# Layer 3's self attention: the weights' sums held in 8 rows a head, inverted in 128 columns and spread by a 0/1 product

## What is computed

```python
g = sigmoid(hidden_states @ Wg + bg)
res = (1.0 - Z_I) * maximum(1.0 - Z_I - Z_J, 0.0) + Z_I * minimum(1.0 - Z_I + Z_J, 1.0)
scope = clip(power(base, 1.0 - g) + 2.0 - abs_ij, 1e-32, 1.0)
log_pen = log(maximum(res * scope, 1e-32))
scores = einsum('bhqd,bhkd->bhqk', q, k) / sqrt(HEAD_DIM) + log_pen[:, None]
probs = softmax(scores, axis=-1)
ctx = einsum('bhqk,bhkd->bhqd', probs, v)
x = layernorm(x + ctx)
```

## Time and profile before

| What | Value |
|---|---|
| median of 3 runs | 2808.49 us (2806.22 to 2809.91) |
| the profiled execution's own time | 2809.17 us |
| its span, first to last instruction | 2807.3 us |
| mean granted TensorE clock | 0.928 |
| PE busy | 2396.4 us (85%) |
| PE weight loads busy | 1887.2 us (67%) |
| DVE busy | 1402.2 us (50%) |
| ACT busy | 871.3 us (31%) |
| POOL busy | 675.7 us (24%) |
| reciprocals of this stage (L2341) | 32, from 2159.3 to 2421.4 us, 55.8 us in all |

### The profile page before, as it was taken

One profiled execution on the slowest core, in us unless ns is written; L12 is line 12 of the kernel. 1 busy time (PEld: TensorE's weight loads), 2 busy tenths in 40 slices (PEclk: granted clock), 3 DMA queues, 4 the chain that ended last, 5 costly groups with the idle time before them and its releaser, 6 DMA issues. The chain is left out here.

```text
span 2807.3 us, 53068 instructions
## 1 busy us (share of the span) xinstructions
PE 2396.4 (85%) x20565; PEld 1887.2 (67%) x20565; DVE 1402.2 (50%) x2857; ACT 871.3 (31%) x1510; POOL 675.7 (24%) x1006
## 2 busy tenths in 40 slices
PE   6959999669889899899889979947977879589992
PEld 2947777434578655799868866626846767479992
DVE  3246666686468631121157756752155988621114
ACT  1124333564234311011122224402234655212223
POOL 0932222241123200122212211102311322123332
PEclk9879999999999999999989989968988999889996
DMA  9020000100020000588710011014510000179994
GB/s 349 1 86 1 0 0 1 32 1 0 12 74 2 32 0 0 221 312 317 254 31 0 0 49 40 2 32 123 166 34 5 2 2 3 43 265 328 325 324 153
DMA packets 163573, 254.28 MB, mean 91 GB/s; under 512 B 17744, under 2 KB 124368, under 8 KB 163152
## 3 DMA queue, kind: packets, MB, share of 16 engines
q1 hardware_dynamic: 154192, 230.92, 24.0%
q0 software_dynamic: 9216, 21.06, 2.8%
HBM read 220.29 MB, written 31.13 MB: 90 GB/s over the span
## 5 line engine op out<-in xcount | busy, mean ns | idle before, releaser
L3225 PE MATMUL te_pU<-te_xsT,te_wu 128*128 128x128 f32 x1952 | 234.9, 277 | 1.7 <-DMA te_wg<-in_L_ffn_gate 1.0
L3225 PEld LDWEIGHTS te_pU<-te_xsT,te_wu 128*128 128x128 f32 x1952 | 232.4, 194 | 5.6 <-issue 2.5
L3246 PE MATMUL te_pY<-te_wd,te_hT 128*128 128x256 f32 x976 | 220.8, 379 | 0.0
L3246 PEld LDWEIGHTS te_pY<-te_wd,te_hT 128*128 128x128 f32 x976 | 180.7, 190 | 22.0
L1123 PE MATMUL x_pB<-early,x_xlT 128*128 128x384 f32 x384 | 137.4, 502 | 4.7 <-DVE x_qn L1350 3.0
L3266 ACT ACTIVATE te_hT<-te_pU 128x512 f32<-128x512 f32 x78 | 46.6, 597 | 242.1 <-PE te_pU L3225 242.1
L3284 DVE COPY te_ys<-te_pY 128x256 f32<-128x256 f32 x61 | 25.9, 425 | 162.8 <-PE te_pY L3246 162.8
L3279 DVE TENSOR_TENSOR te_hT<-te_pU,te_sg 128x512 f32<-128x512 f32 x44 | 30.4, 692 | 149.5 <-ACT te_sg L3264 149.5
L2292 DVE TENSOR_REDUCE x_mx<-x_pR 128x8 f32<-128x1024 f32 x64 | 78.3, 1224 | 52.9 <-PE x_pR L2076 51.1
L3264 ACT ACTIVATE te_sg<-te_pG 128x512 f32<-128x512 f32 x44 | 26.3, 597 | 251.3 <-PE te_pG L3225 251.3
L1123 PEld LDWEIGHTS x_pB<-early,x_xlT 128*128 128x128 f32 x384 | 71.1, 195 | 47.7 <-issue 5.2
(11 more groups left out here) (630 smaller groups left out, 5818.7 us busy)
## 6 DMA issues: line engine op xcount, KB each, us to landing
te_wu<-in_L_ffn_w_upT SPq DMA_DIRECT2D x39, 1024.0 KB, 6.6
te_wd<-in_L_ffn_w_downT SPq DMA_DIRECT2D x39, 1024.0 KB, 7.4
te_wu<-in_L_ffn_up SPq DMA_DIRECT2D x22, 1024.0 KB, 4.9
te_wg<-in_L_ffn_gate SPq DMA_DIRECT2D x22, 1024.0 KB, 7.0
te_wd<-in_L_ffn_down SPq DMA_DIRECT2D x22, 1024.0 KB, 7.9
moe_first<-in_L_ffn_W SPq DMA_DIRECT2D x8, 1024.0 KB, 8.8
xs_slots<-zeros SPq DMA_DIRECT2D x1, 5120.0 KB, 23.5
ys_slots<-zeros SPq DMA_DIRECT2D x1, 5120.0 KB, 35.5
```

Of the source, the lines that this page charges most:

```text
L3225: ins = pe.matmul(out[g][:, m, :], w[:, k, bass.ts(PER * g + m, P)], xsT[:, k, :], start=(k == 0), stop=(k == KD - 1))
L3246: ins = pe.matmul(pY[u][:, 0, :], hT[:, k, :], wd[u][:, k, :], start=(k == 0), stop=(k == KH - 1))
```

## The change

In a part with a penalty, each head's sum stands in 8 rows in place of 16. The 32 rows of a group then hold four heads, and all 16 heads fit into `pO[:, 1, 0, :]`, 128 rows by 128 queries. `attend_sums_in_parts` does this with the same number of products, 16 a block, of the same shape. VectorE inverts these 128 columns (`invert`). TensorE multiplies the inverse by a constant 0/1 matrix (`spread_sums`), two products, which puts each head's inverse back into its 16 rows, over both halves t of `pO[:, 1]`. ScalarE copies them to SBUF (`inverse`), since VectorE's product also reads the values in PSUM, and VectorE multiplies (`normalise_spread`), now after the second maximum. The two constants are loaded with `PenaltyWeights`, and TensorE waits for these.

```diff
@@ class PenaltyWeights
+        self.part_ones, self.spread = self.take(KD * PAIR, ROWS), self.take(KD, P)
+        self.load(sp, self.part_ones, a["c_part_ones"])
+        self.load(sp, self.spread, a["c_spread"])
@@ tensor
+                if p.penalty is not None:
+                    pen.wait(pe)
+            def attend_sums_in_parts(b):
+                for c in range(KD * PAIR):
+                    t, i = c // PAIR, c % PAIR
+                    for g in range(P // ROWS):
+                        ins = pe.matmul(pO[bass.ts(g, ROWS), 1, 0, :], pen.part_ones[:, c, :],
+                                        Pr[b % 2][g // NH][:, g % NH, KD * (1 - i) + t, :], start=(c == 0),
+                                        stop=(c == KD * PAIR - 1))
+                ins.then_inc(o_ready, 1)
+
+            def spread_sums(b):
+                since(pe, o_inverted, b)
+                for t in range(KD):
+                    ins = pe.matmul(pO[:, 1, t, :], pen.spread[:, t, :], R[:, 0, :], start=True, stop=True)
+                ins.then_inc(o_spread, 1)
...
                 scores(n, 1)
+                if live(n - LAG - 1) and part(n - LAG - 1).penalty is not None:
+                    spread_sums(n - LAG - 1)
                 if live(n + 1) and part(n + 1).own:
                     projections(n + 1)
...
                 if live(n - LAG):
-                    attend_sums(n - LAG)
+                    if part(n - LAG).penalty is not None:
+                        attend_sums_in_parts(n - LAG)
+                    else:
+                        attend_sums(n - LAG)
@@ scalar
                     exponentials(n - 1, 0)
+                if live(n - LAG - 1) and part(n - LAG - 1).penalty is not None:
+                    since(act, o_spread, n - LAG - 1)
+                    since(act, oT_ready, n - LAG - 2)
+                    act.copy(inverse[:], pO[:, 1, :, :]).then_inc(spread_copied, 1)
                 if live(n + 1) and part(n + 1).own:
                     query(n + 1)
@@ vector
+            def invert(b):
+                since(dve, o_ready, b)
+                if part(b).penalty is not None:
+                    since(dve, o_spread, b - 1)
+                    ins = dve.reciprocal(R[:, 0, :], pO[:, 1, 0, :])
+                else:
+                    ins = dve.reciprocal(R[:], pO[:, 1, :, :])
+                ins.then_inc(o_inverted, 1)
+
+            def normalise_spread(b):
+                since(dve, spread_copied, b)
+                since(dve, y_ready, b - 2)
+                dve.tensor_tensor(oT[b % 2][:], pO[:, 0, :, :], inverse[:], ALU.mult).then_inc(oT_ready, 1)
...
                 if live(n - LAG - 1):
-                    normalise(n - LAG - 1)
+                    invert(n - LAG - 1)
+                    if part(n - LAG - 1).penalty is None:
+                        normalise(n - LAG - 1)
                 if live(n):
                     maximum(n, 1)
+                if live(n - LAG - 1) and part(n - LAG - 1).penalty is not None:
+                    normalise_spread(n - LAG - 1)
```

More of the change, by code:

```diff
@@ L1892, in attention16 @@
         R = s.sb("R", [P, KD, P])
+        if LAG == 2:
+            inverse = s.sb("inverse", [P, KD, P])
         oT = [s.sb(f"oT{i}", [P, KD, P]) for i in range(2)]
@@ L1921, in attention16 @@
         w_done = [s.sem(f"w_done{i}") for i in range(2)]
-        o_ready, o_inverted = s.sem("o_ready"), s.sem("o_inverted")
+        o_ready, o_inverted, o_spread = s.sem("o_ready"), s.sem("o_inverted"), s.sem("o_spread")
+        spread_copied = s.sem("spread_copied")
+        pen = core.pen
         oT_ready = s.sem("oT_ready")
@@ L2337, in scaled @@
                 dve.tensor_scalar(xn[:], r[:], mv[:, 0:1], rstd[:], ALU.subtract, ALU.mult).then_inc(xn_ready, 1)
+            def invert(b):
[10 more added lines that the diff above has]
+                dve.tensor_tensor(oT[b % 2][:], pO[:, 0, :, :], inverse[:], ALU.mult).then_inc(oT_ready, 1)
             def normalise(b):
-                since(dve, o_ready, b)
-                dve.reciprocal(R[:], pO[:, 1, :, :]).then_inc(o_inverted, 1)
                 dve.wait_ge(o_inverted, b + 1)
@@ L4280, in constants @@
             (np.arange(ROWS)[None, :] // DH == np.arange(PAIR)[:, None]).astype(np.float32)[None], (P, PAIR, ROWS))),
+        "c_part_ones": np.ascontiguousarray(np.broadcast_to(
+            (np.arange(ROWS)[None, :] // 8 == np.arange(4)[:, None]).astype(np.float32)[None], (P, 4, ROWS))),
+        "c_spread": np.stack([(t[:, None] == t[None, :] // ROWS * ROWS + 8 * (2 * m + t[None, :] % ROWS // DH)).astype(np.float32)
+                              for m in range(KD)], axis=1),
         "c_marks": np.ascontiguousarray(np.broadcast_to(
```

## The result

The changed kernel takes 2817.38 us (median of 10 runs, 2815.54 to 2823.19), the kernel before 2807.64 us on the same chip (10 runs, 2804.58 to 2813.81): 9.7 us more, a ratio of 1.0038 with a 95% interval of 1.0029 to 1.0047. The ratio is near that of the means, which differ by 10.5 us. Forecast were 10.4 us more and 2819 us.

What follows compares the result with a forecast made beforehand. A cycle through VectorE and TensorE was taken to close each turn, TensorE having 0.34 us of slack. Terms 0.5 + 0.75 + 9.2 - 1.2 + 1.2 gave +10.4 us, from 2808.49 to 2819, 80% range 2811 to 2827.

Steps and rivals of the forecast that it cites:

- The bound: Turn 8: VectorE and TensorE are nearly full, and TensorE's transposes are only 0.34 us ahead of VectorE.
- The reciprocal: On VectorE: 128 columns in place of 256 take 0.95 us in place of 1.74, 0.79 less a turn.
- The spread's place and price: On TensorE between second scores and projections: 0.66 us waiting for the reciprocal plus 0.60 work, so projections start 1.26 later.
- From there to the put: TensorE's transposes, then VectorE's put of the maxima: after 0.34 us of slack, both come 0.92 late.
- The turn: Turns 5 to 14: 10.50 us a turn in place of 9.58, with VectorE's part after the put held fixed.
- turns 3 and 4: First long turns: +0.5 us in turn 3 for the spread only, +0.75 in turn 4, where TensorE is the bound.
- Turns 5 to 14: The ten long turns with own projections behind a spread: 0.92 us more each, 9.2 in all.
- Turn 15: Next block's projections stand ahead of the second scores, so TensorE has slack; the put comes earlier, -1.2 us.
- Turns 16 to 18: Transposes stand behind attend products that wait for VectorE's product, some 0.5 us later, less at 18; together +1.2 us.
- VectorE as the bound: Rival: all VectorE is spared is gained, 16 turns lose 0.79 us, -12.7, to 2796 us; chance 5%.
- A short reciprocal: Rival: the reciprocal takes about 0.26 us, so TensorE doesn't wait; +2.9 us, to 2811; chance 10%.
- A lower clock: Rival: the longer standstill lowers TensorE's clock; +16 us more, 2835, or 2822 to 2828 for a few turns; chance 8%.

Runs made afterwards that it cites:

- e8: e3 with GpSimd's move of the values at the end of its turn, as in e2; one run of 2802.55 us, turns 5 to 14 of 9.21 us.
- e1: The changed kernel with VectorE's inversion moved ahead of the residual, right behind the first maximum; 2813.53 us, ratio to the kernel before 1.0018.
- e2: The changed kernel with GpSimd's move of the values at the end of its turn in place of the start; 2817.20 us, ratio to before 1.0028.
- e3: The changed kernel without the spread and ScalarE's copy, so inverses are not those of the right heads; 2805.99 us, ratio to before 0.9995.
- e6: The changed kernel with inversion first, GpSimd's values last, transposes before the keys' projections, ScalarE's inverse copy before the exponentials, its values behind keys; 2802.93 us, ratio 0.9979.

## Why the prediction was right, step by step

**The bound.** TensorE's chain of scores, projections and transposes being 0.34 us from setting the turn: e8 measures 0.37.

**The reciprocal.** Predicted 0.95 us from the line through 12 and 256 columns; measured 0.941.

**The spread's place and price.** Measured from the start of the turn's first maximum, the projections start at 3.57 us (2215.71 - 2212.14) in place of 2.38 (2209.74 - 2207.36): 1.19 later, predicted 1.26. The products take 0.55, not 0.60, and the other 0.64 is the waiting, predicted 0.66; the 0.58 that the trace calls idle leaves out the time by which the last score's record reaches into it.

**From there to the put.** Predicted 0.92 late, measured 0.72 (6.64 against 5.92). The projections themselves, to the start of the keys', are 0.10 shorter (1.76 in place of 1.86), since the 0.10 of the group that comes first behind the scores is now the spread's (e1 shows it there without a pause). The prediction put it down to the wait, added it to the spread and left it in the projections too. The last 0.03 lies between the transposes and the put (0.42 in place of 0.45).

**The turn.** Predicted 10.50, measured 10.58. The step that was missing is the weighing: I held VectorE's part after the put fixed, and it grew by 0.27, because it now starts while GpSimd's addition runs (e2). The two errors, 0.20 too much and 0.27 too little, nearly cancel: that the turn came out within 0.08 us is luck in part, while the path and its order were right.

**The sum.** Predicted for turns 3 and 4: +0.5 and +0.75, measured +0.46 and -0.50; the stretch at lower clock in turn 4 of the profile before is not there in the profile after, so this is no test of the term. Turns 5 to 14: +9.2, measured +10.05 (105.84 us against 95.79). Turn 15: -1.2, measured -1.30, by the chain that was given: the product waits 0.23 us for the copy, ends 4.71 us into the turn (predicted 4.73), and the put follows right behind it. Turns 16 to 18: +1.2, measured +1.05 (0.44 + 0.35 + 0.26); in turn 16 the attend products start 4.87 us into the turn in place of 4.38, the 0.5 that was given. Together +10.4 and +9.76. The two profiles' spans differ by 11.7 us: turns 0 to 2 and 19 have -2.3 (turns 1 and 19 ran at 0.84 and 0.82 of the clock before and at 1.00 after), and the remaining 4.2 lie outside these turns, where the change adds no more than two loads. What makes these 4.2 up was not looked into. So the medians' difference of 9.7 us is near the 9.76 of turns 3 to 18 partly by chance; what the change costs is read from turns 5 to 14.

**The rivals.** VectorE as the bound fell with e3 and e8. A short reciprocal fell with its 941 ns. A lower clock: all of turns 5 to 14 ran at 1.00. The reason given against it, pauses under 0.7 us each, was not so: TensorE waits 0.83 us for `a_xn` in turn 8 of the kernel before and 0.73 in the changed one, both at 1.00.

## What to carry to other kernels

When two engines are both nearly full, take the slack of the second one out of the trace, in a turn where it waited for nothing, before making the first one faster: here it was 0.34 us, and 0.80 us taken off the first engine gained 0.37 at most. What is handed to the second engine beyond the slack is paid in full. A small product that waits for another engine costs its wait as well as its length, and both to all that is queued behind it; ask what can go ahead of it, and what need not stand behind it. Once the order fits (e6), the same change pays, if little: 0.45 us a turn, 0.1 to 0.2% of the kernel's time.

## What was not expected

A shift of 0.7 us in one engine's list brought two others into each other's way: GpSimd's addition of 0.73 us and VectorE's weighing, 2.62 us in place of 2.35 for the pair. The weighings of turns 1 to 4 of the kernel before, 2.62 to 3.09 us, were in its trace all along and showed it.
